# Transposing y (second stage) and part of the rounded x (first stage) by DMA in place of TensorE

## The chip, the cores and the metric

One NeuronCore of one Trainium2 chip runs the whole program. The metric is the device time of one execution in microseconds (us); lower is better. The engines are TensorE (PE, with its weight loads as PEld), VectorE (DVE), ScalarE (ACT), GpSimd (POOL) and SyncE (SP), which here does nothing but start DMAs, in the order written; ACT starts a few as well.

## What is computed

A gated cross-attention-like product and a gated feed-forward step, both added to the rows of `x` (2 batches of 1024 rows, 2048 wide), cut to what matters:

```python
# fake_quant(x, s, z) = (clip(round(x / s + z), 0, 255) - z) * s
x = x + tanh(g_xattn[0]) * matmul(fake_quant(layernorm(x)), fake_quant(ctx))       # ctx: 2048 x 2048 per batch
y = layernorm(x)
base   = y @ W_up.T                                                                # 2048 x 2048
top1   = argmax(y @ gate_w.T + expert_bias)                                        # 4 experts
delta  = (y @ lora_A[e].T) @ lora_B[e].T   for e = top1                            # rank 8
x = x + tanh(g_ffn[0]) * (base + delta)
```

## The kernel before

**Tiles.** The 2048 rows are 16 row tiles of 128. A row tile `t` of the first stage is normalised and rounded to integers in bf16 (`q1(t)`, one of two halves of `HL`, 128 x 2048), transposed into `q1T` (four buffers, 16 blocks of 128 x 128), and multiplied with the rounded context `Q` in four chunks of 512 columns (`chunk(t, n)`, 16 matmuls each, L875). The first four row tiles (`HEAD`) go through the chunks side by side while the context still arrives; from tile 4 on the tiles follow one another. DVE adds each chunk to the row tile (`epi`, L599), which lies in one of five buffers and is then stored to `h_scratch` (`store`) except for the last four.

**Second stage.** `y` is a normalised row tile of the result, as two f16 halves, high and low (`HL`, 128 x 2 x 2048 f16, 1 MB), transposed into `YT` (two buffers). The weights are two f16 halves as well, in the arena where the context was. A tile `s` is five chunks of 416 to 418 columns, 48 matmuls each (L920), then five small matmuls of the expert part (L927). The weights were scaled by a power of two per input column; `wback` undoes this on `y`, in the eviction of its transposes.

**Transposes before.** All are matmuls against an identity on TensorE: `transposes(t)` (L853, 16 for a row tile of `x`) in PSUM banks `TR`, evicted by ACT (`evac`, L377, two of them for t >= 4), and `y_transposes(s, g)` (L912, four groups of 8 for a row tile of `y`), evicted by DVE with the factor `wback` (`yT_out`, L645).

**What sets the order.** There is no scheduler: each engine has its instructions in the order of the code, and semaphores. In the first stage ACT and DVE work in `period(p, a, b, c)`, one for each row tile p from 4 on; a, b and c are the rounding of three context tiles (`ctx_round(3p+8)` to `ctx_round(3p+10)` on ACT, L385, `ctx_clip` of the same on DVE, L609) for p = 4 to 7, and work on the weights for p = 8 to 14. `quant(p+2)` (ACT, L358) and `clip(p+2)` (DVE, L592) make `q1(p+2)`; `evac(p+1)` lies behind `quant(p+2)` on ACT. SP's list mixes `ctx_tile`, `row`, `store` and `load_w`; a `store(t)` waits for `epi(t, 3)`. A chunk on TensorE needs a free PSUM bank, that is the `epi` of the sixth chunk before it. In the second stage DVE runs, per tile s, `route(s)`, then `moments`, `norm(s+1)` (L588) and `y_low(s+1)` (L636), with `y_high(s+1)` (L413) on ACT between them, and then `epi2(s, c)` (L693). On ACT `z_out(s)`, which waits for TensorE's second chunk of the tile, lies ahead of the square root that `norm(s+1)` needs.

Of the kernel before, what the change touches and what calls it, by code (L numbers as in the profile page):

```python
# [11 lines left out]
P = 128  # L12
# [6 lines left out]
def build(nc, x, ctx, w, b_t, scal, out):  # L19
# [17 lines left out]
    KEEP = 4  # L37
    HALF = KT // 2
# [7 lines left out]
    o_t = out.rearrange("(t p) d -> t p d", p=P)  # L46
    h_t = nc.dram_tensor("h_scratch", (TILES - KEEP, P, D), F32).ap()
# [8 lines left out]
    with es:  # L56
# [12 lines left out]
        YT = sb("rows_T", [P, 2, KT, 2, P], F16)  # L69
# [4 lines left out]
        Braw = S1[0:ZR, 0:D]  # L74
        arena_bf = arena[:, :].bitcast(BF16)
        arena_i16 = arena[:, :].bitcast(I16)
        q1T = YT[:, :, :, :, :].rearrange("p a k h m -> p (a k h m)").bitcast(BF16).rearrange(
# [99 lines left out]
        s_yh = sem("y_high"); s_yl = sem("y_low"); s_yt = sem("yT_group"); s_ye = sem("yT_out")  # L177
        s_m2 = sem("chunk2_done"); s_dl = sem("delta_done"); s_rt = sem("route_step"); s_zs = sem("z_stack_ready")
# [22 lines left out]
        def Xt(u):  # L201
            return Xc(u, 0, D)
# [10 lines left out]

        @block.sync
        def _(sp):
# [52 lines left out]
            for c in (10, 11, 12, 13, 16, 17, 14, 15, 18, 19):  # L268
                ctx_tile(c)
            store(0)  # L270
            store(1)
# [8 lines left out]
            row(8)  # L280
            ctx_tile(23)
# [3 lines left out]
            ctx_tile(24)  # L285
            ctx_tile(25)
# [4 lines left out]
            ctx_tile(27)  # L291
            ctx_tile(28)
# [4 lines left out]
            ctx_tile(30)  # L297
            ctx_tile(31)
# [5 lines left out]
            row(12)  # L304
            load_w(3)
            store(8)
            row(13)
            load_w(4)
            load_w(5)
            store(9)  # L310
            row(14)
            load_w(6)
            load_w(7)
            store(10)
            row(15)
            load_w(8)
            load_w(9)
            load_w(10)
            store(11)
            for i in range(11, KT + 2):  # L320
                load_w(i)
# [5 lines left out]
            for s in range(KEEP + 1, TILES):  # L327
                row(TILES + s)
# [18 lines left out]
        def _(act):  # L347
# [6 lines left out]
            def quant(t):  # L354
                act.wait_ge(s_sb, t + 1)
                if t >= 2:
                    act.wait_ge(s_tr, 2 * (t - 1))
                A(q1_i16(t), Xt(t), ACT.Relu, bias=L(t, "qb"), scale=L(t, "qs")).then_inc(s_qi, 1)  # L358

                with act.If_ne(flag2, 0):  # L360
                    act.wait_ge(s_q1, t + 1)
                    if t >= 1:
                        act.wait_ge(s_tr, 2 * t)
# [8 lines left out]
            def evac(t):  # L372
                for g in range(1 if t < HEAD else 2):
                    act.wait_ge(s_tr, 2 * t + g + 1)
                    if t >= 4:
                        act.wait_ge(s_mm, place[(t - 4, NCH - 1)] + 1)
                    A(q1T[:, t % 4, GROUP * g:GROUP * (g + 1), :].rearrange("p k m -> p (k m)"),  # L377
                      TR[g].bitcast(BF16), ACT.Copy).then_inc(s_ev, 1)
# [26 lines left out]
            def y_high(s):  # L405
                act.wait_ge(s_norm, s + 1)
                if s == 0:
                    act.wait_ge(s_tr, 2 * TILES)
                else:
                    act.wait_ge(s_yt, 4 * s)  # L410
                    act.wait_ge(s_yl, s)
                u = TILES + s
                A(HL[:, 0, :], Xt(u), ACT.Identity, bias=L(u, "nmr"), scale=L(u, "rstd")).then_inc(s_yh, 1)  # L413
# [21 lines left out]
            ctx_round(0)  # L435
            evac(0)
            ctx_round(1)
            sqrt(1)
            ctx_round(2)
            quant(1)  # L440
# [23 lines left out]
            evac(4)  # L464

            def period(p, a, b, c):
# [37 lines left out]
        def _(dve):  # L504
# [67 lines left out]
            def norm(s):  # L572
# [15 lines left out]
                v.tensor_scalar(T[:, 0:D], Xt(u), L(u, "mean"), L(u, "rstd"), ALU.subtract, ALU.mult).then_inc(s_norm, 1)  # L588
# [43 lines left out]
            def y_low(s):  # L632
                dve.wait_ge(s_yh, s + 1)
                if s >= 1:
                    dve.wait_ge(s_yt, 4 * s)
                v.tensor_tensor(HL[:, 1, :], T[:, 0:D], HL[:, 0, :], ALU.subtract).then_inc(s_yl, 1)  # L636
# [388 lines left out]
```

## Time and profile before

| | |
|---|---|
| time, median of 3 runs | 1028.18 us (1027.31 to 1029.14) |
| profiled execution, its own time | 1028.02 us |
| its span | 1026.2 us |
| TensorE busy | 972.0 us, 95% |
| DVE, ACT busy | 460.6 us, 230.3 us |
| DMA | 119.57 MB, mean 117 GB/s |

The span is what the profile covers; the execution's own time is 1.8 us more. The first stage lasts to about 296 us, then the weights' last half is finished and the first tile of the second stage is made beside it, and from 344 us on fifteen tiles of the second stage follow one another on TensorE alone. A busy share of 95% says that TensorE is the engine to look at, not that all of its work is needed.

### The profile page before, as it was taken

Reading aid. Unit: us, or ns where it says so; the run is one execution under the profiler, and the core shown is the slowest. Engines: PE = TensorE matmul, PEld = TensorE weight load, DVE = VectorE, ACT = ScalarE, POOL = GpSimd, SP = SyncE. Lnnn points to the kernel's source line nnn. Section 1 sums busy time; section 2 is a strip of 40 time slices with the busy share of each in tenths; the row PEclk is TensorE's granted clock in tenths of the full one; section 3 lists DMA queues with packets and bytes.
Section 4 is the critical chain, followed back from the end, with each engine's and each line's share of the span. In section 5 each row is a group of like instructions: output and inputs, shape, how many; then the busy total and the mean of one; then the engine's idle time right before and its main releaser. Section 6 shows DMA issues by size and latency. Waiting matters only on the chain.

```text
span 1026.2 us, 13127 instructions
## 1 busy us (share of the span) xinstructions
PE 972.0 (95%) x5728; PEld 531.3 (52%) x5728; DVE 460.6 (45%) x885; ACT 230.3 (22%) x192; POOL 2.3 (0%) x16
## 2 busy tenths in 40 slices
PE   2899799899899999999999999999999999999997
PEld 1444344444355555555555555555555555555554
DVE  6764565766577542342534233252424325242401
ACT  6584657575633000000000000000000000000000
POOL 0000000000000000000000000000000000000000
PEclk9999999999899999999999999999999999999999
DMA  9968967677534202021020202112020210101011
GB/s 373 420 240 328 402 259 274 200 246 289 221 139 143 82 1 83 1 82 61 22 82 1 83 1 82 42 42 82 2 82 1 82 42 1 42 1 42 1 42 42
DMA packets 16445, 119.57 MB, mean 117 GB/s; under 512 B 1952, under 2 KB 1952, under 8 KB 1952
## 3 DMA queue, kind: packets, MB, share of 16 engines
q1 hardware_dynamic: 14080, 101.90, 26.1%
q10 hardware_dynamic: 2304, 16.78, 4.0%
q8 instruction: 48, 0.79, 0.3%
q14 instruction: 13, 0.11, 0.0%
HBM read 89.31 MB, written 29.36 MB: 116 GB/s over the span
## 4 chain that ended last, share of the span: by engine, by line
PE 74%; DMA 11%; ACT 5%; DVE 5%; issue 3%; SPq 1%; ACTq 0%; DVEq 0%
PE bank L920 62%; PE bank L875 7%; PE bank L912 3%; DMA arena<-in_ctx 2%; ACT arena L385 2%; DMA rows<-in_x 2%; DMA normed<-in_w 2%; DMA h_scratch<-rows 2%; DVE arena L629 2%; DMA stage<-in_ctx 1%; DMA stage<-in_w 1%; PE bank L927 1%; ACT rows_T L377 1%; DVE bn L545 1%; ACT halves L358 1%
## 5 line engine op out<-in xcount | busy, mean ns | idle before, releaser
L920 PE MATMUL bank<-arena,rows_T 128*128 128x416 f16 (+1 forms) x3840 | 686.6, 339 | 2.2 <-DVE arena L629 1.2
L920 PEld LDWEIGHTS bank<-arena,rows_T 128*128 128x128 f16 x3840 | 370.6, 97 | 300.5 <-issue 4.6
L875 PE MATMUL bank<-arena,rows_T 128*128 128x512 bf16 x1024 | 235.5, 390 | 30.2 <-ACT rows_T L377 18.4
L875 PEld LDWEIGHTS bank<-arena,rows_T 128*128 128x128 bf16 x1024 | 100.7, 100 | 157.6 <-issue 21.0
L693 DVE SCALAR_TENSOR_TENSOR rows<-bank,derived,rows 128x416 f32<-128x416 f32 (+2 forms) x80 | 48.4, 641 | 228.9 <-PE bank L927 228.9
L419 ACT ACTIVATE z_stack_T<-bank 96x128 fp32r<-96x128 f32 x16 | 4.4, 274 | 600.7 <-PE bank L934 600.7
L545 DVE BATCH_NORM_STATS2 bn<-rows 128x6 f32<-128x512 f32 x124 | 76.5, 680 | 10.7 <-DMA rows<-in_x 8.6
L645 DVE TENSOR_TENSOR rows_T<-bank,wback 128x1024 f16<-128x1024 f16 x64 | 75.0, 1216 | 0.2 <-DVE z_stack L675 0.2
L659 DVE SCALAR_TENSOR_TENSOR route<-bank,derived,scal 128x4 f32<-128x4 f32 x16 | 3.5, 221 | 115.9 <-PE bank L920 115.8
L599 DVE SCALAR_TENSOR_TENSOR rows<-bank,derived,rows 128x512 f32<-128x512 f32 x60 | 44.4, 747 | 20.9 <-PE bank L875 20.8
L636 DVE TENSOR_TENSOR halves<-normed,halves 128x2048 f16<-128x2048 f32 x16 | 36.7, 2292 | 30.3 <-ACT halves L413 30.3
L385 ACT ACTIVATE arena<-arena,scal,derived 128x2048 int16<-128x2048 f32 x22 | 45.2, 2084 | 10.2 <-DMA arena<-in_ctx 10.2
L413 ACT ACTIVATE halves<-rows,ln 128x2048 f16<-128x2048 f32 x16 | 33.5, 2095 | 39.7 <-DVE normed L588 39.7
L609 DVE TENSOR_SCALAR arena<-arena,derived 128x2048 bf16<-128x2048 int16 x32 | 24.0, 750 | 37.0 <-ACT arena L385 37.0
L554 DVE RECIPROCAL ln<-ln 128x1 f32<-128x1 f32 x32 | 5.1, 160 | 66.3 <-ACT ln L352 66.3
L912 PE MATMUL bank<-ident_h,halves 128*128 128x128 f16 x512 | 34.3, 220 | 0.2 <-DVE rows_T L645 0.2
L358 ACT ACTIVATE halves<-rows,ln 128x2048 int16<-128x2048 f32 x15 | 31.3, 2087 | 4.8 <-DVE ln L569 4.8
L912 PEld LDWEIGHTS bank<-ident_h,halves 128*128 128x128 f16 x512 | 29.0, 98 | 6.2 <-issue 5.0
L853 PE MATMUL bank<-ident_bf,halves 128*128 128x128 bf16 x256 | 17.7, 225 | 15.2 <-DVE halves L592 15.2
L629 DVE SCALAR_TENSOR_TENSOR arena<-stage,wscale,arena 128x2084 f16<-128x2084 f32 x11 | 26.1, 2384 | 8.3 <-ACT arena L403 8.2
L927 PE MATMUL bank<-b_stack,z_stack_T 96*128 96x416 f32 (+2 forms) x80 | 29.1, 432 | 0.4 <-ACT z_stack_T L419 0.4
L377 ACT ACTIVATE rows_T<-bank 128x1024 bf16<-128x1024 bf16 x28 | 27.1, 1010 | 8.9 <-PE bank L853 8.9
(82 smaller groups left out, 271.9 us busy)
## 6 DMA issues: line engine op xcount, KB each, us to landing
arena<-in_ctx SPq DMA_DIRECT2D x22, 1024.0 KB, 17.7
stage<-in_w SPq DMA_DIRECT2D x17, 1042.0 KB, 6.2
out<-rows ACTq DMA_DIRECT2D x16, 1024.0 KB, 3.9
rows<-in_x SPq DMA_DIRECT2D x15, 1024.0 KB, 9.9
rows<-h_scratch SPq DMA_DIRECT2D x12, 1024.0 KB, 4.8
h_scratch<-rows SPq DMA_DIRECT2D x11, 1024.0 KB, 8.3
stage<-in_ctx SPq DMA_DIRECT2D x10, 1024.0 KB, 10.4
normed<-in_w SPq DMA_DIRECT2D x7, 1042.0 KB, 6.6
```

Of the source, the lines that this page charges most:

```text
L358: A(q1_i16(t), Xt(t), ACT.Relu, bias=L(t, "qb"), scale=L(t, "qs")).then_inc(s_qi, 1)
L377: A(q1T[:, t % 4, GROUP * g:GROUP * (g + 1), :].rearrange("p k m -> p (k m)"), TR[g].bitcast(BF16), ACT.Copy).then_inc(s_ev, 1)
L385: A(Qc(c, True), buf, ACT.Relu, bias=z2, scale=V["rs2"]).then_inc(s_cr, 1)
L545: v.bn_stats(bn[:, u % 2, i, :], Xc(u, i * 512, (i + 1) * 512)).then_inc(s_bn, 1)
L599: v.scalar_tensor_tensor(out=xs, in0=bank[ROT[g % 6]][:, :], scalar=V["coef"], in1=xs, op0=ALU.mult, op1=ALU.add).then_inc(s_epi, 1)
L629: v.scalar_tensor_tensor(out=W(n, 1), in0=wbuf[k][:, :], scalar=wa[:, n:n + 1], in1=W(n, 0), op0=ALU.mult, op1=ALU.subtract).then_inc(s_lo, 1)
L645: v.tensor_tensor(dst, src, back, ALU.mult).then_inc(s_ye, 1)
L693: v.scalar_tensor_tensor(out=xs, in0=bank[c][:, a - CUT[c]:b - CUT[c]], scalar=V["gs"], in1=xs, op0=ALU.mult, op1=ALU.add).then_inc(s_e2, 1)
L875: mm = mmul(bk, q1T[:, t % 4, kt, :], Q(b, n, kt), start=(kt == 0), stop=(kt == KT - 1 and not slow), skip_group_check=slow)
L912: mm = nc.tensor.transpose(TR[g % 2].bitcast(F16)[:, i * P:(i + 1) * P], HL[:, h, k * P:(k + 1) * P], idh[:, :])
L920: mm = mmul(bank[c][:, 0:b - a], YT[:, s % 2, kt, yh, :], W(kt, wh, a, b), start=(first and kt == kts[0] and yh == 0 and wh == 0), stop=False,
L927: mmul(bank[c][:, a - CUT[c]:b - CUT[c]], zT[:, :].bitcast(F32R), Bst[:, a - EXT:b - EXT], start=False, stop=True, skip_group_check=True). ...
```

## The change

From its fifth row tile on (t >= 4) `q1(t)` is transposed by one DMA transpose on SP's queue (0.5 MB, `turn_q1`), written into SP's list; the matmuls, the evictions on ACT and their waits go. In the second stage the tiles s >= 2 (`BY_PE`) are transposed by one DMA transpose of 1 MB, both halves at once. As there is no eviction left that could apply `wback`, the factor is taken into `norm`: `wback` is written to HBM as a row, read back into all partitions (`WR`), and `norm` multiplies with it; `rstd` moves into `y_high` and `y_low`. The first two tiles of the second stage stay on TensorE. In ACT's `period`, `b` stands behind `quant` now.

```diff
+    BY_PE = 2
+    wrow_d = nc.dram_tensor("w_back_row", (KT, P), F32).ap()
...
-        YT = sb("rows_T", [P, 2, KT, 2, P], F16)
+        YT = sb("rows_T", [P, 2, 2, KT, P], F16)
...
+        def turned(t):
+
+            return (s_tr, 2 * (t + 1)) if t < HEAD else (s_dx[t % 2], 16 * ((t - HEAD) // 2 + 1))
...
+            def turn_q1(t):
+
+                sp.wait_ge(s_q1, t + 1)
+                sp.wait_ge(s_mm, place[(t - 4, NCH - 1)] + 1)
+                sp.dma_start_transpose(q1T[:, t % 4], q1(t)).then_inc(s_dx[t % 2], 16)
...
             store(4)
             ctx_tile(24)
+            turn_q1(7)
             ctx_tile(25)
             ctx_tile(26)
...
-            for s in range(KEEP + 1, TILES):
-                row(TILES + s)
+            sp.wait_ge(s_wc, 1)
+            sp.dma_start(wrow_d.rearrange("k p -> p k"), wc[:, :],
+                         allow_slow_non_contiguous=True).then_inc(s_wr0, 16)
+            sp.wait_ge(s_wr0, 16)
+            sp.wait_ge(s_lo, KT)
+            sp.dma_start(WR, wrow_d.rearrange("k p -> (k p)").unsqueeze(0).to_broadcast([P, D])).then_inc(s_wr, 16)
+            for s in range(BY_PE, TILES):
+                if s + 3 < TILES:
+                    row(TILES + s + 3)
+                sp.wait_ge(s_yl, s + 1)
+                sp.wait_ge(s_m2, 5 * (s - 1))
+                sp.dma_start_transpose(YT[:, s % 2].rearrange("p h k m -> p (h k) m"),
+                                       HL[:, :, :].rearrange("p h d -> p (h d)")).then_inc(s_dt, 16)
...
             def period(p, a, b, c):
                 a()
                 if p + 2 < TILES:
                     sqrt(p + 2)
-                b()
                 if p + 2 < TILES:
                     quant(p + 2)
-                evac(p + 1)
+                b()
                 c()
...
+                    v.scalar_tensor_tensor(out=T[:, 0:D], in0=Xt(u), scalar=L(u, "mean"), in1=WR, op0=ALU.subtract,
+                                           op1=ALU.mult).then_inc(s_norm, 1)
...
+                    v.scalar_tensor_tensor(out=HL[:, 1, :], in0=T[:, 0:D], scalar=L(TILES + s, "rstd"), in1=HL[:, 0, :],
+                                           op0=ALU.mult, op1=ALU.subtract).then_inc(s_yl, 1)
...
             def tile2(s):
-                nxt = s + 1 < TILES
-                pe.wait_ge(s_ye, 4 * s + 4)
+                if s < BY_PE:
+                    pe.wait_ge(s_ye, 4 * s + 4)
+                else:
+                    pe.wait_ge(s_dt, 16 * (s - BY_PE + 1))
```

SP's list of the first stage, from the store of row tile 4 to that of row tile 6. `h_scratch` is written by a `store`, `stage` and `arena` get a context tile, `rows` a row tile, `normed` a weight tile. Before:

```order
L228 DMA h_scratch<-rows 128x2048 [waits chunk_out]
L234 DMA stage<-in_ctx 128x2048 [waits ctx_rounded] x2
L234 DMA arena<-in_ctx 128x2048 [waits ctx_rounded]
L224 DMA rows<-in_x 128x2048 [waits row_tile_stored4]
L228 DMA h_scratch<-normed 128x2048 [waits chunk_out]
L234 DMA arena<-in_ctx 128x2048 [waits ctx_rounded]
L234 DMA stage<-in_ctx 128x2048 [waits ctx_rounded] x2
L252 DMA normed<-in_w 128x2084 [waits row_tile_stored5]
L228 DMA h_scratch<-rows 128x2048 [waits chunk_out]
```

Now, the same stretch:

```order
L237 DMA h_scratch<-rows 128x2048 [waits chunk_out]
L249 DMA stage<-in_ctx 128x2048 [waits ctx_rounded]
L243 DMA_TRANSPOSE rows_T<-halves 128x16x128 [waits chunk_done,q1_ready]
L249 DMA stage<-in_ctx 128x2048 [waits ctx_rounded]
L249 DMA arena<-in_ctx 128x2048 [waits ctx_rounded]
L233 DMA rows<-in_x 128x2048 [waits row_tile_stored4]
L237 DMA h_scratch<-normed 128x2048 [waits chunk_out]
L249 DMA arena<-in_ctx 128x2048 [waits ctx_rounded]
L243 DMA_TRANSPOSE rows_T<-halves 128x16x128 [waits chunk_done,q1_ready]
L249 DMA stage<-in_ctx 128x2048 [waits ctx_rounded] x2
L267 DMA normed<-in_w 128x2084 [waits row_tile_stored5]
L237 DMA h_scratch<-rows 128x2048 [waits chunk_out]
```

A transpose that waits for `q1_ready` (the clip on DVE) now stands between the first and the second context load of a row tile.

TensorE's list for one tile of the second stage. Before (the `ident_h` rows are the transposes of the next tile's y):

```order
L920 MATMUL bank<-arena,rows_T 128x416 x96
L934 MATMUL bank<-ident_f,z_stack 96x128
L920 MATMUL bank<-arena,rows_T 128x416 x48
L927 MATMUL bank<-b_stack,z_stack_T 128x380
L927 MATMUL bank<-b_stack,z_stack_T 128x416 x2
L912 MATMUL bank<-ident_h,halves 128x128 x16
L920 MATMUL bank<-arena,rows_T 128x418 x48
L927 MATMUL bank<-b_stack,z_stack_T 128x418
L912 MATMUL bank<-ident_h,halves 128x128 x16
L920 MATMUL bank<-arena,rows_T 128x418 x48
L927 MATMUL bank<-b_stack,z_stack_T 128x418
```

Now:

```order
L966 MATMUL bank<-arena,rows_T 128x416 x96
L980 MATMUL bank<-ident_f,z_stack 96x128
L966 MATMUL bank<-arena,rows_T 128x416 x48
L973 MATMUL bank<-b_stack,z_stack_T 128x380
L973 MATMUL bank<-b_stack,z_stack_T 128x416 x2
L966 MATMUL bank<-arena,rows_T 128x418 x48
L973 MATMUL bank<-b_stack,z_stack_T 128x418
L966 MATMUL bank<-arena,rows_T 128x418 x48
L973 MATMUL bank<-b_stack,z_stack_T 128x418
```

The two groups of 16 transposes are gone; the products are the same.

## Rows read from the trace of the kernel before

**Rows 1.** The page: the span, and busy time, share and instructions of TensorE.
```profile
span 1026.2 us, 13127 instructions
PE 972.0 (95%) x5728; PEld 531.3 (52%) x5728; DVE 460.6 (45%) x885; ACT 230.3 (22%) x192; POOL 2.3 (0%) x16
```

**Rows 2.** Timeline of TensorE, one tile of the second stage: start, length, instructions.
```profile
389.55 17.06 PE L920 MATMUL bank<-arena,rows_T 128*128 128x416 f16 x96
...
415.55 1.07 PE L912 MATMUL bank<-ident_h,halves 128*128 128x128 f16 x16
416.45 8.64 PE L920 MATMUL bank<-arena,rows_T 128*128 128x418 f16 x48
...
425.12 1.07 PE L912 MATMUL bank<-ident_h,halves 128*128 128x128 f16 x16
426.03 8.66 PE L920 MATMUL bank<-arena,rows_T 128*128 128x418 f16 x48
...
434.72 1.58 PE L920 MATMUL bank<-arena,rows_T 128*128 128x416 f16 x8
```

**Rows 3.** Waits: who waited for whom, us in total, times, longest.
```profile
PE bank L875 <- ACT rows_T L377: 18.4, 8, 4.0
```

**Rows 4.** Timeline of TensorE, first stage; in brackets the idle time before.
```profile
127.42 8.75 PE L875 MATMUL bank<-arena,rows_T 128*128 128x512 bf16 x32 [3.23 <-ACT rows_T L377]
136.01 1.06 PE L853 MATMUL bank<-ident_bf,halves 128*128 128x128 bf16 x16
136.91 7.07 PE L875 MATMUL bank<-arena,rows_T 128*128 128x512 bf16 x32
...
262.37 9.88 PE L875 MATMUL bank<-arena,rows_T 128*128 128x512 bf16 x32 [4.05 <-ACT rows_T L377]
...
292.04 3.62 PE L875 MATMUL bank<-arena,rows_T 128*128 128x512 bf16 x16
```

**Rows 5.** Windows: busy time of PE, PEld, DVE, ACT, POOL, then PEclk, DMA share, GB/s.
```profile
260.00:280.00 20.00, 17.63 (x81) 7.94 (x82) 10.03 (x23) 12.23 (x13) 0.38 (x1) 0.83 0.60 230
```

**Rows 6.** Timeline of ACT in the period of row tile 5.
```profile
121.38 2.10 ACT L385 ACTIVATE arena<-stage,scal,derived 128x2048 int16<-128x2048 f32 x1 [5.20 <-DMA stage<-in_ctx]
123.38 2.08 ACT L358 ACTIVATE halves<-rows,ln 128x2048 int16<-128x2048 f32 x1
125.36 1.91 ACT L377 ACTIVATE rows_T<-bank 128x1024 bf16<-128x1024 bf16 x2
127.17 2.09 ACT L385 ACTIVATE arena<-stage,scal,derived 128x2048 int16<-128x2048 f32 x1
```

**Rows 7.** Timeline of SP, DMA issues from the store of row tile 4 on.
```profile
112.59 0.33 SPq L228 DMA_DIRECT2D h_scratch<-rows  x1
112.96 1.38 SPq L234 DMA_DIRECT2D stage<-in_ctx  x2
...
130.74 0.33 SPq L228 DMA_DIRECT2D h_scratch<-normed  x1
...
165.69 0.33 SPq L228 DMA_DIRECT2D h_scratch<-rows  x1
```

**Rows 8.** Timeline of DVE: an `epi` near the first stage's end, and a `y_low`.
```profile
257.16 0.74 DVE L599 SCALAR_TENSOR_TENSOR rows<-bank,derived,rows 128x512 f32<-128x512 f32 x1
...
408.18 1.34 DVE L588 TENSOR_SCALAR normed<-rows,ln 128x2048 f32<-128x2048 f32 x1
411.69 2.29 DVE L636 TENSOR_TENSOR halves<-normed,halves 128x2048 f16<-128x2048 f32 x1 [2.16 <-ACT halves L413]
```

**Rows 9.** Groups by line: busy us and mean ns of one, then idle before.
```profile
L592 DVE TENSOR_SCALAR halves<-halves,derived 128x2048 bf16<-128x2048 int16 x16 | 12.0, 750 | 11.4 <-ACT halves L358 11.4
```

**Rows 10.** DMA issues: count, KB each, median us from issue to landing.
```profile
out<-rows ACTq DMA_DIRECT2D x16, 1024.0 KB, 3.9
rows<-h_scratch SPq DMA_DIRECT2D x12, 1024.0 KB, 4.8
...
normed<-in_x SPq DMA_DIRECT2D x1, 1024.0 KB, 25.7
```

More of the change, by code:

```diff
@@ L177, in build @@
         s_yh = sem("y_high"); s_yl = sem("y_low"); s_yt = sem("yT_group"); s_ye = sem("yT_out")
+        s_wc = sem("w_back_scale"); s_wr0 = sem("w_back_row_parked"); s_wr = sem("w_back_row_loaded")
+        s_dt = sem("y_transposed_by_dma"); s_dx = [sem(f"q1_transposed_by_dma{i}") for i in range(2)]
         s_m2 = sem("chunk2_done"); s_dl = sem("delta_done"); s_rt = sem("route_step"); s_zs = sem("z_stack_ready")
@@ L269, in _ @@
                 ctx_tile(c)
+            turn_q1(4)
             store(0)
+            turn_q1(5)
             store(1)
@@ L280, in _ @@
             row(8)
+            turn_q1(6)
             ctx_tile(23)
@@ L291, in _ @@
             ctx_tile(27)
+            turn_q1(8)
             ctx_tile(28)
@@ L297, in _ @@
             ctx_tile(30)
+            turn_q1(9)
             ctx_tile(31)
@@ L304, in _ @@
             row(12)
+            turn_q1(10)
             load_w(3)
@@ L307, in _ @@
             row(13)
+            turn_q1(11)
             load_w(4)
@@ L311, in _ @@
             row(14)
+            turn_q1(12)
             load_w(6)
@@ L315, in _ @@
             row(15)
+            turn_q1(13)
             load_w(8)
@@ L319, in _ @@
             store(11)
-            for i in range(11, KT + 2):
+            turn_q1(14)
+            load_w(11)
+            load_w(12)
+            turn_q1(15)
+            for i in range(13, KT + 2):
                 load_w(i)
@@ L372, in evac @@
             def evac(t):
[L373 to L378, printed above, removed]
+                act.wait_ge(s_tr, 2 * t + 1)
+                A(q1T[:, t % 4, 0:GROUP, :].rearrange("p k m -> p (k m)"), TR[0].bitcast(BF16),
+                  ACT.Copy).then_inc(s_ev, 1)
             def ctx_round(c):
@@ L435, in _ @@
             ctx_round(0)
+            sqrt(1)
             evac(0)
             ctx_round(1)
-            sqrt(1)
+            quant(1)
             ctx_round(2)
-            quant(1)
             ctx_round(3)
@@ L825, in _ @@
                     y_low(s + 1)
-                for c in range(3):
+                for c in range(5):
                     epi2(s, c)
-                for g in range(4):
-                    if g == 2:
-                        epi2(s, 3)
-                    if s + 1 < TILES:
-                        yT_out(s + 1, g)
-                epi2(s, 4)
         @block.tensor
@@ L839, in half_out @@
             def half_out(t, g):
-                if g and t < HEAD:
-                    pe.wait_ge(s_evb, t + 1)
-                else:
-                    pe.wait_ge(s_ev, t + 1 if t < HEAD else HEAD + 2 * (t - HEAD) + g + 1)
+                pe.wait_ge(s_evb if g else s_ev, t + 1)
             def transposes(t):
@@ L869, in chunk @@
                     pe.wait_ge(s_epi, g - 5)
-                half_out(t, 0)
-                half_out(t, 1)
+                if t < HEAD:
+                    half_out(t, 0)
+                    half_out(t, 1)
+                else:
+                    pe.wait_ge(*turned(t))
                 for kt in range(KT):
@@ L888, in stage1 @@
                             transposes(t + 1)
-                        if n == NCH - 1 and t == 0:
-                            transposes(HEAD)
                 for t in range(HEAD, TILES):
@@ L893, in stage1 @@
                         chunk(t, n, slow)
-                        if n == 1 and t + 1 < TILES:
-                            transposes(t + 1)
                         if n == 1 and t == TILES - 1:
```

52 lines of the change are left out of this document (29 added, 23 removed).

## The prediction

> **What bounds the kernel now.** I began with the busy times of the page [rows 1]: TensorE works 972.0 of 1026.2 us. So I looked at what it does. The timeline of a second-stage tile [rows 2] shows no gap: the tile starts at 389.55, the next at 434.72, a period of 45.17 us, in which two groups of 16 transposes stand in line with the products. There each instruction on TensorE is worth its time. Next the waits [rows 3]: in the first stage TensorE stands 18.4 us, in 8 waits, for ACT's evictions of the transposes, and the timeline [rows 4] shows where, once per row tile from tile 5 on. After a wait of over 2 us the next 32 matmuls take 8.75 us in place of 7.07, and 9.88 after the longest; in that stretch the granted clock is 0.83 on the mean of 20 us [rows 5], so part of it was spent at the lower of the two levels (1.2 GHz in place of 2.4).
>
> Why is ACT late? Its timeline for the period of row tile 5 [rows 6] starts with a context tile that it waited 5.20 us for, a DMA. That DMA was issued at 112.96, right behind the store of row tile 4 at 112.59 [rows 7], and its rounding starts at 121.38, 8.4 us later. From there on: rounding, quant, evict, rounding of the third context tile (it has long arrived, because SP issued it in the same breath), clip, last `epi`, and the next store at 130.74. So the first stage is a loop over store, DMA, ACT, DVE, store again, in which TensorE isn't at all. Its period from 112.59 to 165.69 is 53.1 / 3 = 17.7 us, while a row tile's chunks need 4 x 3.46 = 13.8 us on TensorE (7.07 less the overlap for 32 matmuls, 136.91 to the next start). This decides what the change may bring there: freeing TensorE gives nothing back while the loop sets the pace.
>
> **Second stage, what goes.** The group at 415.55 delays the products to 416.45, that at 425.12 to 426.03 [rows 2]: 0.90 + 0.91 = 1.81 us per tile. 14 tiles (s = 2 to 15) lose them: -25.3 us. The y evictions on DVE go too, worth nothing, DVE idles there.
>
> **Second stage, what comes.** `y_low` of the next tile ends at 411.69 + 2.29 = 413.98 [rows 8], 24.4 us into the tile. `norm` has a second f32 input now; the nearest row is `y_low` itself, 2.29 us against norm's 1.34, so +0.95: the transpose can start 25.4 us into a tile of 45.17 - 1.81 = 43.36 us. It has 18.0 us. The trace has no DMA transpose and no copy within SBUF. Nearest for 1 MB: 3.9 us for a store and 4.8 for a load in this stage [rows 10]; the slowest 1 MB of the trace took 25.7 us, queued behind others. I take 4 to 8 us: the queue is nearly empty here, so the quick rows are nearer. Then all of it is hidden, as is SP's wait for `y_low`: behind it stands only the load of the row tile three ahead. Without that cover each us over 18 costs 14. The detour of `wback` through HBM is hidden likewise; should it make `norm(2)` late, it has the same 18 us, once.
>
> In sentences apart: the Trainium skill, "VectorE: DVE Perf Modes", section "The three transpose paths", gives 1309 ns for one 128x128 block by DMA. The 32 blocks of a y tile would then be 41.9 us if they followed one another, and the second stage would have a period of 25.4 + 41.9 = 67.3 us. The same skill, "DMA: Bandwidth & Descriptors", section "Latency and other measured facts", has 261 GB/s for a DMA transpose, 4.0 us for 1 MB. No row here can tell between them.
>
> **First stage, what goes.** 12 groups of transposes, each 136.91 - 136.01 = 0.90 us [rows 4]: 10.8 us. The waits for the evictions, 18.4 us [rows 3]. The slow matmuls after them: 1.68 us for the three of 8.75 (one is shown) and 2.81 for the one of 9.88, 7.9 us. Were TensorE the bound, that is -37.1 us. It isn't, so I go by the loop.
>
> **First stage, what comes.** In the list of SP, the second context load of a period now stands behind `turn_q1(p+2)`, which waits for `clip(p+2)`, which on DVE comes after the first context tile of that period. Two DMAs that flew together now follow one another. Counted from the arrival at 121.38: rounding 2.10 and `ctx_clip` 0.75, `clip` 0.75 [rows 6, 9] (quant is done before, by ACT's new order), so the transpose is issued at +3.7. The load behind it lands 4.8 us later by itself [rows 10], plus what the 0.5 MB ahead of it holds the rings, half of 3.9, so about 2.0: +10.5. Then rounding 2.1, clip 0.75, `epi` 0.74 [rows 8]: the next store at +14.1. Before it came at 130.74 - 121.38 = 9.36. So +4.7 us in each of the periods of tiles 5, 6 and 7; if the transpose holds the rings 6 us, +8.7. In period 4 the same rule puts one context load and one row load about 8 us later, most of it in DMA backlog; I take +2. Sum at the end of the context: +16 us (up to +28).
>
> In the periods 8 to 13 the loop is the same with weight tiles. The transpose is ready when SP comes to it, so it adds its 2 us of rings, and ACT is relieved of the evict, 1.91 us: I take -0.5 a period, -3 in all. At the end the gain comes out: TensorE waits 4.05 us at 262.37 and then crawls [rows 4]; without that, and without the group of transposes, 4.05 + 2.81 + 0.9 = 7.8 us. At most it runs up to the sixth `epi` before it: `epi(13,0)` ends at 257.9 [rows 8], six chunks of 3.46 and the 1.8 us of y transposes end at 280.5, where it now ends at 295.7 [rows 4], -15 us. The last weight loads, which `wback` needs, lie between; I take -12. The stage in all: +16 - 3 - 12 = +1, from -8 to +15. With nothing lost to the order of SP it is -37.
>
> The tail of the first stage (last weights, first y tile) is bound by ACT, DVE and loads and keeps its length.
>
> **Sum.** Against the profiled execution, 1028.0 us (span 1026.2 and 1.8 around it, 0.2 from the median of the runs): 1028.0 - 25.3 + 1 = 1003.7, I say 1004. Its own range is 988 to 1019.
>
> **The rivals.**
> *The y transpose doesn't fit (slower).* Place: TensorE's wait ahead of a tile s >= 2. It decides at 18.0 us for 1 MB; the gain of 24 us is gone at 18.0 + 24 / 14 = 19.7. At the slowest row, 25.7 us, the period is 51.1, +5.9 against now, 14 times: +83; the x transposes at half of that, 12.9 us, are 11 more than I took in three periods and half as much in the six with weights: +66 with the +1. That gives 1177. For it: no DMA of this trace takes data apart into 2-byte elements, so nothing here says that this is as quick as whole rows. Against: the 1 MB transfers that don't queue take 3.9 and 4.8 us [rows 10]. Chance 0.23. By the Trainium skill's price of a block, above, y alone would cost 14 x (67.3 - 45.2) = 309 us.
> *The order of SP eats the gain.* y is hidden, but an x transpose holds the rings some 6 us: +28 in the context periods, +2 in each of six weight periods and -12 at the end, +28: 1031; with half of that, 1017. For it: the first stage's loop goes through SP. Against: half the bytes of a load. Chance 0.13 for 1019 to 1035.
> *The first stage is freed.* The loop closes up because loads that follow singly land sooner, and TensorE becomes the bound: 1028.0 - 25.3 - 37.1 = 966; half of it 984. For it: 18.4 us of waits name the evictions. Against: those evictions waited for DMA themselves. Chance 0.10 for 965 to 988.
> The forecast has 0.54.
>
> **How the numbers follow.** A measurement tells 0.2% (2 us) from no change. Faster: forecast, freed, and a third of the SP case, 0.54 + 0.10 + 0.04 = 0.68. Same: 0.04, from the SP case. Slower: the rest of it and the y case, 0.28. For 8 in 10 the range takes in the freed stage and the SP case, and the nearest part of the y case: 966 to 1060.
>
> **What would show it.** Right: second-stage period 43.4 us, no wait of TensorE for a DMA; y transposes landing in under 18 us; in the first stage stores of row tiles 4 to 7 some 22 us apart and ACT's third context round waiting for its DMA. Wrong: TensorE waiting for `rows_T<-halves` ahead of each tile (y rival); stores still 18 us apart (freed). What would break the forecast most is the duration of one DMA transpose, which no row of this trace bounds from above by its kind.

## The result, and the profile after

The changed kernel takes 1046.66 us (1045.05 to 1047.95, 4 runs), the kernel before, in the same rounds, 1027.94 (1027.31 to 1029.14, 4 runs): 1.018 times as long, 95% interval 1.0162 to 1.0198. The forecast was 1004, 24 us faster; it is 18.7 us slower instead.

The page of the changed kernel (profiled execution 1047.24 us): span, busy time, DMA packets, and the group of the first stage's matmuls, which are L925 now (L875 before), as the products are L966 (L920 before). They answer to [rows 1].
```profile
span 1045.4 us, 11747 instructions
...
PE 947.8 (91%) x5066; PEld 499.0 (48%) x5088; DVE 411.8 (39%) x829; ACT 208.1 (20%) x168; POOL 2.3 (0%) x16
...
DMA packets 101398, 141.50 MB, mean 135 GB/s; under 512 B 86784, under 2 KB 86784, under 8 KB 86784
...
L925 PE MATMUL bank<-arena,rows_T 128*128 128x512 bf16 x1002 | 242.6, 402 | 61.8 <-DMA rows_T<-halves 28.8
```
TensorE works 24 us less in a span that is 19 us longer: it has work taken away and stands still more.

The waits of the changed kernel: who waited for whom, us in total, times, longest. They answer to [rows 3].
```profile
ACT arena L427 <- DMA stage<-in_ctx: 44.6, 7, 11.4
...
PE bank L925 <- DMA rows_T<-halves: 28.8, 7, 8.6
```
The 18.4 us for the evictions are gone, and TensorE waits 28.8 us for the new transposes. The first row is the larger one: ACT waits 44.6 us for context tiles, where the same view of the kernel before has 15.7:
```profile
ACT arena L385 <- DMA stage<-in_ctx: 15.7, 3, 6.2
```

Second stage first, since it went as forecast. Timeline of TensorE, one tile, answering to [rows 2]:
```profile
389.57 17.04 PE L966 MATMUL bank<-arena,rows_T 128*128 128x416 f16 x96
...
415.55 8.66 PE L966 MATMUL bank<-arena,rows_T 128*128 128x418 f16 x48
...
424.24 8.67 PE L966 MATMUL bank<-arena,rows_T 128*128 128x418 f16 x48
...
432.95 2.29 PE L966 MATMUL bank<-arena,rows_T 128*128 128x416 f16 x12
```
The period is 432.95 - 389.57 = 43.38 us, and no row carries a wait. The two y steps on DVE, answering to [rows 8], then the transpose on SP in the same tile, and its line's durations (issue in ns, min, median, max; landing in us):
```profile
408.18 2.35 DVE L638 SCALAR_TENSOR_TENSOR normed<-rows,ln,stage 128x2048 f32<-128x2048 f32 x1
412.60 2.35 DVE L690 SCALAR_TENSOR_TENSOR halves<-normed,ln,halves 128x2048 f16<-128x2048 f32 x1 [2.07 <-ACT halves L460]
```
```profile
414.98 4.77 SPq L372 DMA_TRANSPOSE rows_T<-halves  x1
```
```profile
L372 SPq DMA_TRANSPOSE rows_T<-halves x14: 4736/4827/5406, 415.0 to 978.9; - x14
...
DMA to landing us min/median/max: 6.7/6.7/8.3
```
Issued 25.4 us into the tile, landed 6.7 us later, needed at 43.4: 11 us to spare.

The loss is in the first stage. Timeline of SP from row tile 4 on, answering to [rows 7]:
```profile
116.14 2.01 SPq L243 DMA_TRANSPOSE rows_T<-halves  x1
...
119.61 0.43 SPq L237 DMA_DIRECT2D h_scratch<-rows  x1
120.09 0.65 SPq L249 DMA_DIRECT2D stage<-in_ctx  x1
137.63 1.76 SPq L243 DMA_TRANSPOSE rows_T<-halves  x1
139.44 1.14 SPq L249 DMA_DIRECT2D stage<-in_ctx  x1
...
148.84 0.33 SPq L237 DMA_DIRECT2D h_scratch<-normed  x1
...
171.13 0.33 SPq L237 DMA_DIRECT2D h_scratch<-rows  x1
```
and ACT in that period, answering to [rows 6]; in brackets the idle time before:
```profile
134.06 2.09 ACT L427 ACTIVATE arena<-stage,scal,derived 128x2048 int16<-128x2048 f32 x1 [3.12 <-DMA stage<-in_ctx]
145.28 2.09 ACT L427 ACTIVATE arena<-stage,scal,derived 128x2048 int16<-128x2048 f32 x1 [9.12 <-DMA stage<-in_ctx]
```
Behind the context load of 120.09 SP stands for 17 us at the transpose of row tile 7, whose clip on DVE comes after the context tile that has only just been asked for; the next context load goes out at 139.44, where before it went out in the same breath. The store that came 18.2 us after the last one now comes after 29.2.

The same loop for whole periods, in both kernels and in each experiment: distances between the stores of row tiles 4 to 11 in us, the end of the first stage's matmuls, and the first products of the second tile of the second stage, "stage 2" (all from the timelines of SP and TensorE).

| kernel | store 4 | 4-5 | 5-6 | 6-7 | 7-8 | 8-9 | 9-10 | 10-11 | end | stage 2 |
|---|---|---|---|---|---|---|---|---|---|---|
| before | 112.6 | 18.2 | 18.2 | 16.7 | 18.1 | 17.6 | 17.8 | 23.2 | 295.7 | 344.4 |
| after | 119.6 | 29.2 | 22.3 | 23.0 | 16.0 | 17.2 | 23.5 | 31.8 | 337.9 | 389.6 |
| y_only | 114.6 | 18.1 | 18.0 | 16.7 | 19.8 | 17.7 | 17.6 | 22.4 | 296.1 | 348.0 |
| wait_only | 115.3 | 22.1 | 20.9 | 20.7 | 15.9 | 17.6 | 17.6 | 23.5 | 305.4 | 354.7 |
| late | 122.6 | 16.5 | 15.2 | 16.1 | 17.0 | 18.6 | 18.7 | 33.6 | 304.4 | 355.6 |
| x_on_act | 123.2 | 14.7 | 21.9 | 15.8 | 15.7 | 16.5 | 25.6 | 29.4 | 312.7 | 363.6 |
| from6 | 116.7 | 27.9 | 23.3 | 22.1 | 17.0 | 16.6 | 22.5 | 31.8 | 334.2 | 385.3 |
| to12 | 118.9 | 27.9 | 23.8 | 22.2 | 17.6 | 16.6 | 22.5 | 22.9 | 322.8 | 376.2 |
| mid_late | 119.7 | 16.6 | 15.3 | 15.7 | 17.5 | 18.3 | 18.9 | 23.7 | 296.2 | 346.3 |
| act_order | 114.7 | 14.9 | 14.9 | 14.7 | 17.5 | 16.5 | 21.2 | 28.8 | 294.5 | 342.8 |
| y_act8 | 112.8 | 15.4 | 14.9 | 14.7 | 17.5 | 17.6 | 17.6 | 22.6 | 285.9 | 336.7 |
| mid10 | 119.5 | 17.0 | 15.2 | 16.2 | 17.5 | 17.9 | 19.1 | 22.5 | 297.4 | 347.3 |
| extra_turns | 127.5 | 22.4 | 18.7 | 17.2 | 18.0 | 17.6 | 20.8 | 26.3 | 323.5 | 371.5 |
| extra_both | 128.0 | 29.1 | 23.9 | 24.9 | 16.1 | 17.9 | 20.7 | 28.2 | 346.0 | 394.3 |

The first stage ends 42.2 us later than before: 7.0 by the store of tile 4, 21.5 in the three context periods, 11.9 from store 7 to store 11, 1.9 from there to the end (they sum to 42.3; rounding). In the weight periods SP, and at the end TensorE, look like this:
```profile
204.29 5.16 SPq L243 DMA_TRANSPOSE rows_T<-halves  x1
...
220.70 5.24 SPq L243 DMA_TRANSPOSE rows_T<-halves  x1
225.98 1.35 SPq L267 DMA_DIRECT2D stage<-in_w  x2
...
283.23 7.75 SPq L243 DMA_TRANSPOSE rows_T<-halves  x1
291.02 0.58 SPq L267 DMA_DIRECT2D stage<-in_w  x1
```
```profile
293.17 22.69 PE L925 MATMUL bank<-arena,rows_T 128*128 128x512 bf16 x94 [8.59 <-DMA rows_T<-halves]
```
In this kernel the issue of an x transpose takes SP 4.7 to 7.8 us where SP issued a 1 MB load or store in the 1.3 us before it (four times), and 1.3 to 2.8 us elsewhere (eight times); what stands behind it waits; at 293.17 TensorE has waited 8.59 us for one of them.

The windows of the first stage: busy time of PE, PEld, DVE, ACT and POOL, then PEclk, DMA share and GB/s. Before, the same two windows had PEclk 0.96 and 0.98.
```profile
120.00:200.00 80.00, 53.40 (x205) 21.56 (x210) 31.96 (x76) 28.77 (x19) 0.00 (x0) 0.83 0.74 255
200.00:340.00 140.00, 105.55 (x463) 46.96 (x471) 82.58 (x165) 61.40 (x54) 0.38 (x1) 0.89 0.69 221
```
With more idle time TensorE's granted clock is lower too (0.83 and 0.89), so more of these stretches was spent at the lower level, 1.2 GHz. In the context periods, where stores and context loads set the pace, I take that as a consequence of the loss and not its source; no run tests it apart.

### The profile page after: what moved, and what is told of

It is laid out like the page before. It is cut to its first block, busy times and chain, and to the rows that moved or that the text cites. A ratio compares the mean times of both kernels' runs of the same rounds, so it can differ in the third digit from the quotient of the medians.

```text
span 1045.4 us, 11747 instructions
## 1 busy us (share of the span) xinstructions
PE 947.8 (91%) x5066; PEld 499.0 (48%) x5088; DVE 411.8 (39%) x829; ACT 208.1 (20%) x168; POOL 2.3 (0%) x16
## 4 chain that ended last, share of the span: by engine, by line
PE 68%; DMA 14%; DVE 7%; ACT 5%; SPq 3%; issue 3%; ACTq 0%; DVEq 0%
PE bank L966 61%; PE bank L925 5%; DMA stage<-in_ctx 4%; DMA stage<-in_w 3%; DMA rows<-in_x 3%; ACT arena L427 3%; SPq L243 2%; DVE arena L680 2%; PE bank L973 1%; DVE bn L590 1%; ACT arena L445 1%; DMA h_scratch<-rows 1%; DMA stage<-in_b_t 1%; DMA rows_T<-halves 1%; DMA arena<-in_ctx 1%
## 5 line engine op out<-in xcount | busy, mean ns | idle before, releaser
L966 PE MATMUL bank<-arena,rows_T 128*128 128x416 f16 (+1 forms) x3840 | 687.4, 339 | 1.1 <-issue 1.0
L966 PEld LDWEIGHTS bank<-arena,rows_T 128*128 128x128 f16 x3840 | 369.8, 97 | 304.7 <-issue 10.2
L925 PE MATMUL bank<-arena,rows_T 128*128 128x512 bf16 x1002 | 242.6, 402 | 61.8 <-DMA rows_T<-halves 28.8
L925 PEld LDWEIGHTS bank<-arena,rows_T 128*128 128x128 bf16 x1024 | 103.2, 102 | 199.2 <-issue 67.8
L590 DVE BATCH_NORM_STATS2 bn<-rows 128x6 f32<-128x512 f32 x124 | 76.5, 680 | 18.7 <-DMA rows<-in_x 16.5
L690 DVE SCALAR_TENSOR_TENSOR halves<-normed,ln,halves 128x2048 f16<-128x2048 f32 x14 | 32.9, 2351 | 29.0 <-ACT halves L460 29.0
L460 ACT ACTIVATE halves<-normed,ln 128x2048 f16<-128x2048 f32 x14 | 28.0, 2002 | 48.6 <-DVE normed L638 48.6
L638 DVE SCALAR_TENSOR_TENSOR normed<-rows,ln,stage 128x2048 f32<-128x2048 f32 x14 | 32.9, 2352 | 0.8 <-DVE ln L623 0.4
L680 DVE SCALAR_TENSOR_TENSOR arena<-stage,wscale,arena 128x2084 f16<-128x2084 f32 x11 | 26.1, 2386 | 14.7 <-ACT arena L445 14.6
L427 ACT ACTIVATE arena<-stage,scal,derived 128x2048 int16<-128x2048 f32 x10 | 20.8, 2089 | 44.6 <-DMA stage<-in_ctx 44.6
L973 PE MATMUL bank<-b_stack,z_stack_T 96*128 96x416 f32 (+2 forms) x80 | 29.1, 432 | 0.4 <-ACT z_stack_T L466 0.4
L445 ACT ACTIVATE arena<-stage,wscale 128x2084 f16<-128x2084 f32 x11 | 22.0, 2021 | 16.7 <-PE bank L925 12.8
L958 PE MATMUL bank<-ident_h,halves 128*128 128x128 f16 x64 | 6.1, 265 | 14.1 <-DVE halves L688 11.3
L900 PE MATMUL bank<-ident_bf,halves 128*128 128x128 bf16 x64 | 5.0, 242 | 15.2 <-DVE halves L643 15.2
```

Of the source, the lines that this page charges most:

```text
L427: A(Qc(c, True), buf, ACT.Relu, bias=z2, scale=V["rs2"]).then_inc(s_cr, 1)
L445: A(W(n, 0), wbuf[k][:, :], ACT.Identity, scale=wa[:, n:n + 1]).then_inc(s_hi, 1)
L590: v.bn_stats(bn[:, u % 2, i, :], Xc(u, i * 512, (i + 1) * 512)).then_inc(s_bn, 1)
L638: v.scalar_tensor_tensor(out=T[:, 0:D], in0=Xt(u), scalar=L(u, "mean"), in1=WR, op0=ALU.subtract, op1=ALU.mult).then_inc(s_norm, 1)
L680: v.scalar_tensor_tensor(out=W(n, 1), in0=wbuf[k][:, :], scalar=wa[:, n:n + 1], in1=W(n, 0), op0=ALU.mult, op1=ALU.subtract).then_inc(s_lo, 1)
L690: v.scalar_tensor_tensor(out=HL[:, 1, :], in0=T[:, 0:D], scalar=L(TILES + s, "rstd"), in1=HL[:, 0, :], op0=ALU.mult, op1=ALU.subtract).the ...
```

## The experiments

All with their ratio to the kernel before, run on the same chip, and its 95% interval. Theory A: only the waits for the clips, in the middle of SP's list, cost time, and a transpose is as cheap as a half load. Rival C: the transposes themselves hold SP's queue or the rings. (Rival B, for `y_only` alone: the y transposes cost something that the period doesn't show.) Later a theory D joined A and C, and a theory G took the order of ACT's work apart from the DMA.

**y alone, the waits alone, the order, another queue.** `y_only` is the kernel before with the second stage's part of the change.
```diff
-        YT = sb("rows_T", [P, 2, KT, 2, P], F16)
+        YT = sb("rows_T", [P, 2, 2, KT, P], F16)
...
+                sp.wait_ge(s_yl, s + 1)
+                sp.wait_ge(s_m2, 5 * (s - 1))
+                sp.dma_start_transpose(YT[:, s % 2].rearrange("p h k m -> p (h k) m"),
```


> The first stage as before the change (x transposed on TensorE, SP's list as before), only the second stage with y by DMA. The second stage of the changed kernel ran at a period of 43.38 us against 45.17, so theory A (all of the loss is the first stage) expects 1028 - 25 = 1003 us, up to 1006 if the 3 us by which the stretch between the stages grew comes with y. Rival B (the y transposes cost something that the period does not show) expects over 1010.

Measured: 1006.04 us against 1027.07, 0.9796 [0.9779, 0.9813]. That is theory A's upper end, and rival B falls. The second stage's part gives -21.0 us. Of the 25.3 us some 3.6 go to the stretch before the second tile of the second stage: first-stage matmuls end at 296.1, where they ended at 295.7, and that tile starts at 348.0 and not at 344.4. The whole loss, and more, is then the first stage's: 1046.66 - 1006.04 = 40.6 us.

`wait_only` is the kernel before, in which SP waits for the clips at the places where the changed kernel does, and issues nothing there; TensorE still transposes.
```diff
+            def turn_q1(t):
+
+                sp.wait_ge(s_q1, t + 1)
+                sp.wait_ge(s_mm, place[(t - 4, NCH - 1)] + 1)
...
             ctx_tile(22)
             row(8)
+            turn_q1(6)
             ctx_tile(23)
             row(9)
```


> The kernel before the change with nothing but the waits of the x transposes at their places in SP's list (wait for the clip, wait for the chunk); no DMA transpose is issued. Theory A (what costs is that later loads stand behind the transpose's wait) expects the first stage to grow by at least half of the 42 us that it grew by in the changed kernel, stores of row tiles 4 to 7 over 21 us apart, and 1045 to 1065 us in all. Rival C (what costs is the transposes' own issue and time on the rings) expects 1028 to 1033.

Measured in a single run: 1038.29 us against 1027.07, +11, below what A expected (1045 to 1065) and above what C did (1028 to 1033). The context periods grow to 22.1, 20.9 and 20.7, +10.7 in all; the weight periods don't grow. So the wait is a cause, of about a quarter of the 40.6 us.

`late` is the changed kernel with the x transposes later in SP's list: in the context periods behind the context and row loads, in most weight periods behind the first weight load. ACT's order is the changed kernel's.
```diff
             store(4)
             ctx_tile(24)
-            turn_q1(7)
             ctx_tile(25)
             ctx_tile(26)
             row(10)
+            turn_q1(7)
```


> The changed kernel with the x transposes moved in SP's list: in the context periods behind all loads of their period, in the weight periods behind the first weight load (the transposes of tiles 14 and 15 likewise). Same transposes, same bytes. Theory A expects the stores of row tiles 4 to 7 to be 17 to 19 us apart again and the first stage to end at 285 to 300 us, 990 to 1006 us in all. Rival C expects little change, 1035 to 1047.

Measured: 1015.12 us, 0.9892 [0.9875, 0.9908]. The context periods are short now, 15 to 16.5 us (`act_order`, below, shows that ACT's order alone makes them 14.8). That is 31.5 us better than the changed kernel, but still 9 slower than `y_only` and above theory A's 990 to 1006, far below C's 1035 to 1047: neither holds alone. Its SP timeline shows what is left:
```profile
116.56 6.03 SPq L243 DMA_TRANSPOSE rows_T<-halves  x1
122.63 0.58 SPq L237 DMA_DIRECT2D h_scratch<-rows  x1
...
198.10 7.10 SPq L243 DMA_TRANSPOSE rows_T<-halves  x1
```
The store of row tile 4 goes out without a gap behind a transpose whose issue takes 6.03 us, at 122.63, 10 us later than before. In the last periods the weights lag as well (10-11 takes 33.6); there ACT's order has a part in it, as `act_order` shows below.

`x_on_act` issues the x transposes from ACT's queue, each at the end of a period, so that no load of SP is behind them.
```diff
+                act.wait_ge(s_q1, t + 1)
+                act.wait_ge(s_mm, place[(t - 4, NCH - 1)] + 1)
+                act.dma_start_transpose(q1T[:, t % 4], q1(t)).then_inc(s_dx[t % 2], 16)
...
                 c()
+                if p + 2 < TILES:
+                    turn_q1(p + 2)
```


> The changed kernel with the x transposes issued from ACT's queue at the end of each of ACT's periods, none in SP's list in the first stage. Theory A expects about what moving them late in SP's list gives, 990 to 1010 us, with ACT losing 1.3 us or more per issue. Rival C (their time on the rings delays loads whoever issues them) expects 1035 or more.

Measured: 1013.31 us (1007.83 to 1023.45, 8 runs; the profiled one 1021.3), 0.9858 [0.9823, 0.9894]. No better than `late` by more than the scatter, and a little above the 990 to 1010 that A expected. ACT's timeline, and two issues of SP's queue meanwhile:
```profile
94.04 20.02 ACTq L408 DMA_TRANSPOSE rows_T<-halves  x1
114.10 0.20 ACT L379 ACTIVATE ln<-ln 128x1 f32<-128x1 f32 x1 [18.03 <-issue]
...
135.25 3.80 ACTq L408 DMA_TRANSPOSE rows_T<-halves  x1
139.16 2.09 ACT L415 ACTIVATE arena<-arena,scal,derived 128x2048 int16<-128x2048 f32 x1 [2.83 <-issue]
```
```profile
102.80 0.60 SPq L243 DMA_DIRECT2D arena<-in_ctx  x1
107.58 0.33 SPq L233 DMA_DIRECT2D rows<-in_x  x1
```
The issue stops ACT's own work as it stopped SP's. The longest took 20.02 us, and ACT stood 18.03 us for it; the store of row tile 4 came at 123.2, 10.6 us later than before. In these 20 us the DMA engines moved 405 GB/s (window 94 to 114), and SP's queue issued its plain loads in 0.33 to 0.60 us. The transposes from ACT's queue land after 8.5 us on the median, 24.8 at the most.

**Which tiles.** Both are the changed kernel with some tiles' x on TensorE: the first line is `from6`, the second `to12`.
```diff
+    BY_DMA = (6, 7, 8, 9, 10, 11, 12, 13, 14, 15)
...
+    BY_DMA = (4, 5, 6, 7, 8, 9, 10, 11, 12)
```
In both, and in `mid_late`, ACT's order goes with it:
```diff
+                if p + 2 not in BY_DMA:
+                    b()
                 if p + 2 < TILES:
                     quant(p + 2)
-                b()
+                evac(p + 1)
+                if p + 2 in BY_DMA:
+                    b()
```
So `to12` also has the old order of ACT from period 11 on.


> The changed kernel with row tiles 4 and 5 transposed on TensorE as before the change; tiles 6 to 15 by DMA at the changed kernel's places. Theory D (each x transpose in SP's list holds SP and the rings 2 to 8 us wherever loads are under way, on top of the wait) expects the store of row tile 4 back near 114 us from 119.6 and 1037 to 1042 us in all. Rival A (only the wait for the clip costs, and tiles 4 and 5 hardly wait) expects no change, 1045 to 1048.

> The changed kernel with row tiles 13, 14 and 15 transposed on TensorE as before the change. Theory D expects the stores of tiles 10 and 11 some 23 us apart again instead of 31.8 and no wait of TensorE for these tiles' transposes: 1030 to 1038 us. Rival E (the first stage's end is bound by the weight loads alone) expects 1044 to 1048.

Measured: `from6` 1043.78 us, 1.0146 [1.0124, 1.0168], only 2.9 better than the changed kernel, less than theory D expected (the store of tile 4 comes at 116.7, not near 114), so tiles 4 and 5 matter little. `to12` 1031.11, 1.0027 [1.0013, 1.0042], 15.5 better, within theory D's 1030 to 1038. Its last store distance is 22.9 in place of 31.8, and the stretch from store 11 to the end is 4.8 us shorter. Whether the transposes of tiles 13 to 15 cost that or ACT's new order in those periods, this run can't tell, since both went.

`mid_late` puts `from6`, `to12` and `late` together, with y by DMA: tiles 6 to 12 by DMA, late in SP's list.
```diff
+    BY_DMA = (6, 7, 8, 9, 10, 11, 12)
...
             row(10)
+            turn_q1(7)
```


> x transposes by DMA for tiles 6 to 12 alone, placed behind the loads of their period, the rest on TensorE; y by DMA. Both costs of theory D are then small: context and weight periods of 16 to 18 us, the first stage ends at 285 to 295 us, 995 to 1005 us in all, no slower than y alone (1006.0). If the transposes cost their time on the rings everywhere, 1008 to 1015.

Measured: 1004.18 us, 0.9766 [0.9744, 0.9787]. This is `y_only` (1006.04) less 1.9 us: seven x transposes by DMA in the best places found, with ACT's new order up to period 10, are worth next to nothing.

**What the relief is worth.** In the changed kernel ACT quantizes ahead of the second context or weight step of a period. `act_order` gives that order alone to the kernel before, `y_act8` gives it to `y_only` for the periods before 9, `mid10` to `mid_late`'s order with tiles 6 to 10 by DMA.
```diff
-                b()
+                if p >= 9:
+                    b()
                 if p + 2 < TILES:
                     quant(p + 2)
                 evac(p + 1)
+                if p < 9:
+                    b()
```
(`y_act8`; in `act_order` the condition is left out.)

> The kernel before the change with ACT's order alone changed: quant and evict stand ahead of the second context or weight step of each period. Theory D gives this no part in the loss: within 3 us of before, 1025 to 1031. Rival F (ACT's order delays the next load) expects 1033 or more.

> y by DMA, x on TensorE, and ACT's new order (quant and evict ahead of the second step) in the periods of tiles 4 to 8 alone. The order alone made the context periods 14.8 us from 17.7 but lost it again in the weight periods. Theory G (the new order hurts in the weight periods, and the gain comes out if it is left out there) expects the first stage to end at 286 to 291 us and 996 to 1001 us in all. Rival H (the first stage's end is set by the weight loads whatever came before) expects it to end at 294 to 297 us and 1003 to 1007.

> y by DMA; x by DMA for tiles 6 to 10 alone, behind the loads of their periods; ACT's new order in the periods 4 to 8. Theory G expects 994 to 1001 us, rival H 1002 to 1007. If the x transposes gain nothing over ACT's order, it is no faster than the kernel with that order and y alone.

Measured: `act_order` 1026.79 us, 0.9986 [0.9971, 1.0000]: context periods of 14.8 us in place of 17.7, lost again in the weight periods. Its last two distances, from store 9 to store 11, are 21.2 + 28.8 = 50.0 us, where the kernel before has 41.0. `y_act8` keeps the old order there, comes to these periods as early, and has 40.2: so the new order by itself costs some 9 us in this stretch, with no x transpose by DMA at all. `y_act8` is the fastest of all: 999.00 us, 0.9715 [0.9687, 0.9743], 47.7 us faster than the changed kernel and 29.8 than the one before. Its first stage ends at 285.9. `mid10`, the same with five x transposes by DMA, 1002.25, 0.9747 [0.9719, 0.9775]: slower than without them, by 3 us, and above the 994 to 1001 that theory G expected. ACT's period in `y_act8`, to be held against [rows 6]:
```profile
120.91 1.91 ACT L393 ACTIVATE rows_T<-bank 128x1024 bf16<-128x1024 bf16 x2
122.72 4.07 ACT L401 ACTIVATE arena<-stage,scal,derived 128x2048 int16<-128x2048 f32 x2
126.69 2.08 ACT L401 ACTIVATE arena<-arena,scal,derived 128x2048 int16<-128x2048 f32 x1
```
The context roundings stand together behind the eviction, and none waits.

**The DMA alone.** `extra_turns` is the kernel before with 12 DMA transposes of 0.5 MB more, at the places of the changed kernel in SP's list, of the row tile before, whose clip is long done; TensorE's own transposes overwrite what they bring, and ACT's evictions and roundings wait for them. `extra_both` waits for the tile's own clip too (`t + 1` in the first line below). ACT's order is the old one.
```diff
+                sp.wait_ge(s_q1, t)
+                sp.wait_ge(s_mm, place[(t - 4, NCH - 1)] + 1)
+                sp.dma_start_transpose(q1T[:, t % 4], q1(t - 1)).then_inc(s_dx[t % 2], 16)
...
+                if t > HEAD:
+                    act.wait_ge(*extra(t - 1))
...
                         act.wait_ge(s_mm, place[(t - 4, NCH - 1)] + 1)
+                        act.wait_ge(*extra(t))
```


> The kernel before the change (x and y on TensorE) with 12 further DMA transposes of 0.5 MB at the changed kernel's places in SP's list. Each transposes the row tile before (already clipped), so SP hardly waits for it, and the result is overwritten by the true one, which waits until it has landed. What they cost is their issue and their time on the rings alone. Waits alone made 1038.3. Theory D expects the first stage to grow by 15 to 32 us, 1043 to 1060 us in all, most of it at the store of tile 4, and in the periods of tiles 10 and 11. Rival A (only the waits cost) expects 1028 to 1033.

> As the kernel with 12 further transposes, and each also waits for the clip of its own row tile, as in the changed kernel. If the two costs add up, the first stage grows by the sum of both: 1053 to 1070 us. The changed kernel's first stage ended 42 us later than before; if this one's ends no later than 42 us, TensorE's relief from the x transposes bought nothing.

Measured: `extra_turns` 1056.92 us, 1.0283 [1.0251, 1.0314]; `extra_both` 1076.15, 1.0458 [1.0427, 1.0489]. SP in `extra_turns`, then the line's durations:
```profile
116.84 9.43 SPq L239 DMA_TRANSPOSE rows_T<-halves  x1
...
127.50 0.34 SPq L233 DMA_DIRECT2D h_scratch<-rows  x1
127.89 0.92 SPq L245 DMA_DIRECT2D stage<-in_ctx  x1
128.90 11.41 SPq L239 DMA_TRANSPOSE rows_T<-halves  x1
140.36 0.58 SPq L245 DMA_DIRECT2D stage<-in_ctx  x1
```
```profile
L239 SPq DMA_TRANSPOSE rows_T<-halves x12: 2351/5942/11409, 81.5 to 278.1; - x12
...
DMA to landing us min/median/max: 4.4/9.0/13.5
```
So on top of the kernel before, the waits alone cost 11 us, the transposes alone 29, both together 49, 8 above the sum of the two. (`extra_turns` is within theory D's 1043 to 1060, `extra_both` above the 1053 to 1070 expected.) The 29 is rather an upper value for the changed kernel: ACT's waits for the overwritten tiles are in it, and 14.9 of it have come by the store of tile 4, where the changed kernel has lost 7.0. With both paid (+49) and y's part won (-21) the changed kernel would stand at 1055; it stands at 1047. By this rough account, what the relief of TensorE and ACT and ACT's new order gave together is some 8 us, and not the 37 that the relief would be worth were TensorE the bound.

What stays open: what a transpose's long issue waits for. The 20.02 us of `x_on_act` stopped the queue that issued it and not SP's, while other transfers kept the DMA engines at 405 GB/s, and the long issues of the changed kernel stand right behind another DMA's. So what is outstanding matters, on whichever queue it was issued; by what means, no run shows. Open too is how the loss of the weight periods divides: no run has the changed kernel with ACT's old order.

## Why the prediction was wrong

**The second stage** was right in each step: -1.79 us a tile, period 43.38 where 43.36 was forecast, start of the transpose at 25.4 us as forecast, landing in 6.7 us where 4 to 8 were taken. The rival that y doesn't fit didn't come. The Trainium skill's 1309 ns for one block ("VectorE: DVE Perf Modes", "The three transpose paths") would have made 41.9 us of this, were it paid 32 times; the trace has 6.7, for 32 blocks in one instruction. The estimate of 4.0 us from the Trainium skill's 261 GB/s ("DMA: Bandwidth & Descriptors", "Latency and other measured facts"), which it measured on one kernel, is too low by 2.7 us, but of the right kind. One part of the step fell: the passage between the stages doesn't keep its length. The second tile starts 51.7 us after the first stage's end in the changed kernel, 52.0 in `y_only`, and 48.7 before. That is +3.0 to +3.3.

**"So +4.7 us in each of the periods of tiles 5, 6 and 7", "sum at the end of the context: +16 us (up to +28)".** The mechanism was right, and so was its chain (but for a slip of 0.1: 2.10 + 0.75 + 0.75 is 3.6, not 3.7): from the arrival (134.06) to the next store (148.84) the trace has 14.8 us, where +14.1 was forecast. The periods of tiles 6 and 7 came out 4.1 and 6.3 us longer (forecast 4.7 each). What was mis-sized is the way to the arrival: in the period of tile 5 the first context tile came 14.0 us after its issue (120.09 to 134.06), not 8.4. The transpose of tile 6, a context tile, a row tile and the store had been issued in the 4 us ahead of it, which I take for the reason. That period is 11.0 us longer, not 4.7, and the store of tile 4 came 7.0 us late, not 2. Sum: 7.0 + 21.5 = +28.5, where my upper bound stood.

**"It adds its 2 us of rings", "-0.5 a period", periods 8 to 13: "-3 in all".** This step failed: +11.9 us by store 11, where `wait_only`, without transposes, has -2.1. More than all of it lies between stores 9 and 11, 55.3 us where there were 41.0; those before are no longer than they were, though each holds a transpose whose issue takes SP 5.2 us (204.29 and 220.70). Two terms were wrong. I priced a transpose by its bytes, half a load, and not by its issue, behind which the weight load of 225.98 stands: `extra_turns`, with the old order on ACT, has 47.1 in the same stretch, +6.1. And I put the price of ACT's new order in these periods at nothing, without a reason, where `act_order`, without a DMA transpose, has 50.0, +9.0. The two come to +15.1 and the changed kernel has +14.3, so the order is at least as likely a source of this loss as the transposes; they weren't parted in the changed kernel itself.

**"At the end the gain comes out: -12".** This failed too: +1.9. I had the loop end where the context tiles end. But the last x transposes (283.23, 7.75 us) stand between the last weight loads, and TensorE waits up to 8.59 us for them. From store 11 to the end `act_order` takes 51.2 us, `to12`, with tiles 13 to 15 on TensorE, 50.4, `extra_turns` 54.8 and the changed kernel 55.2, which points to the transposes and not to ACT's order. (`late` takes 46.1, behind a store 11 that itself stood behind one.)

**The sum.** In the terms of the prediction: -25.3, then +28.5 + 11.9 + 1.9 = +42.3 in place of +1, and +3 in the passage: 1028.0 - 25.3 + 42.3 + 3.0 = 1048, measured 1047.2 in the profiled execution. (The terms as I gave them, -8 to +15, make a range of 995 to 1018, where I wrote 988 to 1019.) The likeliest of the rivals by its mechanism is "the order of SP eats the gain", which I gave 0.13 and priced at +28 for a hold of 6 us a transpose; the issue held SP 5 to 8 us in three of the six weight periods, near what that rival says, but its -12 at the end failed with mine, and it has nothing of ACT's order. That its +28 for the context periods matches the measured number is luck: the issues there took 1.8 us, and the time went to late context tiles. I had the unknown, a transpose's duration, right by its landing in an empty queue, and took that for its price in a full one.

## What to carry to other kernels

A DMA transpose hides well where its queue is empty and its data are ready long before they are needed: here it takes y off TensorE for 21 us. In a queue that carries the loads of a loop it is a different thing: price it by what stands behind it, in issue time and not in bytes, and never put an item that waits for a late step of the period between two loads of that period. Before relieving an engine, look whether it sets the pace: here the three context periods went from 17.7 to 14.8 us by one order on ACT, with TensorE's transposes kept. And test a change of order that rides along on its own: the same order cost some 9 us in the weight periods, which the gain hid.

## What the runs showed of the hardware

The issue of a DMA transpose keeps the issuing engine's queue busy: 4.7 to 5.4 us for 1 MB in the quiet second stage, and for 0.5 MB from 1.3 us up to 7.7 in the changed kernel, 11.4 in `extra_turns` and 20.0 from ACT's queue in `x_on_act`, against 0.3 to 2.5 us for a 1 MB load. It stopped the queue that issued it; SP's issued plain loads in 0.33 to 0.60 us during those 20.0. It lands in 4.3 us at the least for 0.5 MB; at the most in 9.8, 13.5 and 24.8 us in these three kernels, counted from the start of the issue. The transposes move packets of about 256 bytes: in `extra_turns` the page has 26912 packets under 512 B where the kernel before has 1952, 2080 for each transpose of 0.5 MB.

The write of `wback` to HBM, 8 KB in 4-byte pieces, is slow for its size, 13.4 us to landing; a 1 MB store of `out` takes 3.9. Of the DMA issues of the changed kernel (count, KB each, median us to landing):
```profile
rows_T<-halves SPq DMA_TRANSPOSE x26, 6.7
...
w_back_row<-wback SPq DMA_DIRECT2D x1, 8.0 KB, 13.4
```
